# Cross attention scores: 32-row products per head, or 128-row products with zero-padded queries

## The reference

```python
Q = (x_text @ Wq).reshape(Bb, Tt, H, DH)      # H, DH = 4, 32
K = (x_vision @ Wk).reshape(Bb, Gg, H, DH)
scores = jnp.einsum('bthd,bghd->bhtg', Q, K) / np.sqrt(DH).astype(np.float32)
scores = jnp.where(vision_mask[:, None, None, :], scores, -jnp.inf)
topv, topi = jax.lax.top_k(scores, K_TOP)     # K_TOP = 32
probs = jax.nn.softmax(topv, axis=-1)
```

## Time and profile before

| | us |
|---|---|
| median of 3 runs | 5040.57 (5039.6 to 5043.89) |
| profiled execution | 5041.77, of it the span of instructions 5039.7 |
| TensorE busy | 4324.6 (86%), weight loads 3107.2 (62%) |
| VectorE busy | 4096.0 (81%) |
| ScalarE busy | 2074.3 (41%) |
| GpSimd busy | 2188.5 (43%) |
| mean granted TensorE clock | 0.873 |

### The profile page before, as it was taken

The page is one execution under the profiler, slowest core; times in us unless marked ns, Lnnn a source line. Parts: engine busy times, 40 slices in busy tenths (PEclk is TensorE's granted clock), DMA queues, the critical chain, the costliest instruction groups (busy, mean ns, idle before and its releaser), DMA issues. The chain is left out here.

```text
span 5039.7 us, 70649 instructions
## 1 busy us (share of the span) xinstructions
PE 4324.6 (86%) x28037; PEld 3107.2 (62%) x28066; DVE 4096.0 (81%) x4353; ACT 2074.3 (41%) x3688; POOL 2188.5 (43%) x2260
## 2 busy tenths in 40 slices
PE   8999976578889899899899899887578989898984
PEld 6777753256566566566666666667456666666661
DVE  5666659699999999999999999986256767777767
ACT  3433322144444444444444444431234545444453
POOL 1111116434444376677677677660233333333321
PEclk9999988678888788888888888888789999999996
DMA  2111115300001101021101111013531111111101
GB/s 84 51 45 51 49 49 184 120 17 26 31 28 44 45 28 34 30 65 34 32 30 43 57 34 30 28 53 92 194 103 43 61 44 58 47 58 54 51 26 36
DMA packets 214587, 275.98 MB, mean 55 GB/s; under 512 B 96659, under 2 KB 144403, under 8 KB 210224
## 3 DMA queue, kind: packets, MB, share of 16 engines
q1 hardware_dynamic: 196850, 216.91, 14.2%
q0 software_dynamic: 17408, 54.56, 2.9%
HBM read 186.44 MB, written 84.98 MB: 54 GB/s over the span
## 5 line engine op out<-in xcount | busy, mean ns | idle before, releaser
L1548 POOL TENSOR_TENSOR c_s<-c_s,c_z 128x2048 f32<-128x2048 f32 x128 | 581.6, 4544 | 755.6 <-ACT c_z L1333 755.6
L1488 DVE MAX8 c_top<-c_z 128x8 f32<-128x2048 f32 x384 | 878.8, 2288 | 8.8
L1489 DVE MATCH_REPLACE8 c_z<-c_top,c_z 128x2048 f32<-128x2048 f32 x384 | 873.9, 2276 | 0.0
L1174 PEld LDWEIGHTS c_p_a<-c_diag,c_s 128*128 128x128 f32 x4096 | 593.5, 234 | 238.4 <-ACT c_diag L1345 160.6
L1174 PE MATMUL c_p_a<-c_diag,c_s 128*128 128x128 f32 x4096 | 615.8, 321 | 131.3 <-ACT c_diag L1345 95.0
L1164 PE MATMUL c_p_s<-c_kt,c_qT 32*128 32x512 f32 x1024 | 542.4, 920 | 105.1 <-ACT c_s L1327 103.5
L1868 PE MATMUL f_p_g<-f_hT,f_w 128*128 128x128 f32 x4096 | 538.4, 295 | 70.2 <-ACT f_gT L1968 55.7
L1868 PEld LDWEIGHTS f_p_g<-f_hT,f_w 128*128 128x128 f32 x4096 | 526.9, 211 | 90.7 <-ACT f_gT L1968 58.6
L1876 PE MATMUL f_p_o<-f_w,f_gT 128*128 128x512 f32 x1024 | 481.8, 592 | 0.0
L1327 ACT ACTIVATE c_s<-c_p_s 128x512 f32<-128x512 f32 x512 | 286.9, 595 | 362.3 <-PE c_p_s L1165 360.5
L1164 PEld LDWEIGHTS c_p_s<-c_kt,c_qT 32*128 32x128 f32 x1024 | 185.2, 247 | 345.1 <-ACT c_s L1327 321.2
(11 more groups left out here) (360 smaller groups left out, 7561.4 us busy)
## 6 DMA issues: line engine op xcount, KB each, us to landing
mod_out<-c_fo POOLq DMA_DIRECT2D x32, 512.0 KB, 2.9
f_mr<-mod_out SPq DMA_DIRECT2D x32, 512.0 KB, 4.8
p_ct<-in_ctxT SPq DMA_DIRECT2D x16, 768.0 KB, 4.9
c_vals<-in_ctx SPq DMA_DIRECT2D x4, 3072.0 KB, 12.1
c_kb<-kspec SPq DMA_DIRECT2D x22, 512.0 KB, 4.3
a_xt<-in_xT SPq DMA_DIRECT2D x32, 256.0 KB, 3.1
a_xr<-in_x SPq DMA_DIRECT2D x32, 256.0 KB, 2.6
x<-a_out POOLq DMA_DIRECT2D x32, 256.0 KB, 2.5
```

The lines of the kernel that those rows point to most:

```text
L1174: last = mm(p_a[:, n, :], s[:, h, n * P:(n + 1) * P], diag[:, j % 2, :], start=(h == 0 and n % 4 == 0), stop=(h == NH2 - 1 and n % 4 == 3) ...
L1488: st.link(v.max(best[n], z[:, par, :]))
L1489: last = v.match_replace(z[:, par, :], best[n], z[:, par, :], NEG)
L1548: pool.tensor_tensor(s[:, h, :], s[:, h, :], z[:, j % 2, :], ALU.subtract).then_inc(w_ready, 1)
```

## The change

`qT` gets a dimension for the head: `[P, 2, NH2, P]` in place of `[P, 2, P]`. GpSimd clears all of it at the start of the stage, and ScalarE waits for that once. `copy_q` writes each head's 32 rows into that head's own block, with four copies in place of one, so in a block all rows of the other heads stay zero. The scores of a head are then a product over all 128 rows of its block and of `kt`. The mask's product stays as it is.

```diff
-        qT = m.sb("qT", [P, 2, P])
+        qT = m.sb("qT", [P, 2, NH2, P])
...
-                        mm(p_s[:, i, :], qT[r:r + HS, t % 2, :], kt[r:r + HS, cols], start=True, stop=False)
+                        mm(p_s[:, i, :], qT[:, t % 2, 2 * p + i, :], kt[:, cols], start=True, stop=False)
                         mm(p_s[:, i, :], oneb[r:r + 1, :], mrow[r:r + 1, cols], start=False, stop=True).then_inc(s_done, 1)
...
                 act.wait_ge(q_done, t + 1)
-                a(qT[:, t % 2, :], p_m[:, 1, 0:P], ACT.Copy).then_inc(q_copied, 1)
+                for h in range(NH2):
+                    part = slice(HS * h, HS * h + HS)
+                    last = a(qT[part, t % 2, h, :], p_m[part, 1, 0:P], ACT.Copy)
+                last.then_inc(q_copied, 1)
...
+            act.wait_ge(zeroed, 1)
             copy_q(0)
             copy_s(0, 0)
...
         def _(pool):
+            pool.memset(qT[:], 0.0).then_inc(zeroed, 1)
             pool.wait_ge(core_in, 16 * 3)
```

More of the change, by code:

```diff
@@ L964, in cross @@
          prod_ready, v_ready, fb_ready, g_in, ig_in, rf_done, rf_copied, r_step, rk_read, rv_ready, ri_done,
-         ri_copied) = [
+         ri_copied, zeroed) = [
             m.sem(n) for n in (
@@ L971, in cross @@
                 "prod_ready v_ready fb_ready g_in ig_in rf_done rf_copied r_step rk_read rv_ready ri_done "
-                "ri_copied").split()]
+                "ri_copied zeroed").split()]
         cx_in = [m.sem(f"cx_in{u}") for u in range(2)]
```

## The result

The changed kernel takes 5114.86 us (median of 4 runs, 5112.21 to 5118.91) against 5042.23 us before: a ratio of 1.0145, 95% interval 1.0127 to 1.0162. It is slower by 73 us. The forecast was 5041.1 us with a range of 5036 to 5060 us.

A forecast was written before the change was run, and what follows sets the result against it. VectorE's own passes, 18.80 us a head, were taken to bound the stage. The profiled 5041.77 us plus 0.6 for the lead-in gave 5042.4; the runs' median lies 1.2 lower, so 5041.1 us, range 5036 to 5060.

The forecast's parts named there:

- the serial pair: Score products: two heads one after the other take 2.16 us at full clock, 4.3 us at half, before switches.
- Rows of zeros: Score products, rival A: zero rows don't count and the clock still falls; +425 us, 5465 us, chance 0.08.
- The lead-in: Before the stage's first head: first score group ends at 979.1 us, 0.6 us later; bounds 0 to +8.3 us.
- The end: Last attention products after the last score group: 0, up to -4 us if the clock is up.
- The memset: GpSimd's clearing at the stage's start: 0.6 to 4.9 us long, costing 0 in idleness, at dearest under 1.2 us.
- copy_q: ScalarE's query eviction: four copies for one delay the spectra and group 1 by +0.52 us, bounds 0.51 to 0.83.
- The clock afterwards: Score groups: full clock taken from the 128-row streams, so a group lasts 10.93 us, bounds 9.5 to 12.05.
- the cover named for ScalarE: ScalarE behind copy_q: only copy_a and two heads' exponentials, whose buffers VectorE wants most of 18.80 us later.
- starts at 2243.4 us and ends at 2254.4 us: Group 2 of the score products in one tile: ends 2.7 us ahead of VectorE, so VectorE loses nothing.
- The switches: TensorE between 128 rows and one: four a pair at 0.09 us each, bounds 0 to 0.16; pair 2.52 us.
- late from g = 12.3 us on: Score groups: VectorE is late for group 2 once a group's time g reaches 12.3 us.
- Rival B: TensorE's row switches: at 0.25 us each a group takes 13.5 us; +74 us, 5115 us, chance 0.08.

The follow-up runs named there:

- e2: Changed kernel, four copies kept, with the mask's product widened from one row to 128 rows; 5042.0 us, ratio 0.9998.
- e3: Changed kernel with the edits of e1 and e2 together: one copy of the queries and a 128-row mask product; 5042.2 us, ratio 0.9998.
- e1: Changed kernel with one ScalarE copy of the queries again, GpSimd writing the padded blocks from it; 5084.3 us, ratio 1.0075.
- f1: Changed kernel with one copy of the queries releasing TensorE and the four copies into the blocks following on ScalarE; 5070.0 us, ratio 1.0052.
- f3: e1 with the spectra waiting for GpSimd's padding instead of the copy; 5136.0 us, ratio 1.0183.
- e4: Kernel before with only the four copies and zeroed blocks added, products still of 32 rows; 5146.5 us, ratio 1.0202.
- e5: e4 with one copy of the queries releasing TensorE and the four copies following from SBUF, 32-row products; 5074.8 us, ratio 1.0075.
- e8: e1 with ScalarE evicting group 2 before the exponentials of the next head; 5050.2 us, ratio 1.0017.
- e7: e1 with score products of 64 rows, half of them zero, instead of 128; 5412.5 us, ratio 1.0736.
- e6: Kernel before with its copy of the queries cut into two of 64 partitions each; 5056.5 us, ratio 1.0028.

## Why the prediction was wrong

**What held.** VectorE bounds the stage, and nothing counts until a score group is late: wherever no group is late the heads are 18.80 us apart, and e2 and e3, whose groups take very different times on TensorE, end where the kernel before ends. The overlap of the two heads is lost and the serial pair is 2.16 us with wide products alone (e2). Rows of zeros count as rows. The lead-in grew by 0.4 us (from the first product to the first head 13.81 us instead of 13.40), forecast 0.6. The end changed by -2.5 us, within -4 to 0. The memset took 0.95 us and cost nothing visible. (VectorE's digits are 9 from the 9th to the 26th slice, not from the 8th; nothing hangs on it.)

**What failed first: "copy_q", +0.52 us.** Two things. The size was 1.10 - 0.28 = 0.82 us, my upper bound: the copies of a quarter of the partitions are as long as the whole one (268 against 278 ns). And the step counted these copies only as a later start of group 1. They are also idleness of TensorE ahead of the spectra, just behind two other gaps (1.40 and 0.69 us in this tile, as long as before), and it is there that the clock now falls. The runs show it by itself: 0.46 us, no fall in 29 tiles (e1, f1); 1.29 and 1.58 us, 25 to 28 of 29 (changed, e2, f3), and 22 with 32 rows (e4). Where VectorE waited for it, group 1 took up to 17.25 us instead of 10.93. This term carries the 54.4 us ahead of group 1, and all but 1.5 of the 18.6 us ahead of group 2, where TensorE was late already. The part of the prediction that it overturns is "The clock afterwards", where I took full clock from the 128-row streams and never asked what happens at the spectra ahead of them.

**What was wrong second, but cost nothing here: the cover named for ScalarE.** I wrote that only copy_a and exponentials stand behind copy_q. copy_f and group 1's evictions stand there too, with 0.30 us to spare. In the changed kernel TensorE was later still: ScalarE mostly waited 1.39 us for group 1's first product. With 32 rows and no longer gap the same oversight is worth 34 us (e5).

**What was wrong third: group 2 "starts at 2243.4 us and ends at 2254.4 us".** An early start doesn't bring an early end. ScalarE takes up the evictions 11.2 us ahead of VectorE's need at the earliest, and TensorE's waiting for it costs clock as well. The trace of the kernel before shows this already: where its group 2 starts 16 us ahead, at 1188 us for one, it takes 15.5 us and ends 0.60 us ahead of need. In the changed kernel this was hidden, since TensorE mostly came later than ScalarE. e1 shows the price once the gap is gone, 35.7 us, and e8 takes most of it away.

**The switches.** The cost per head was 0.29 us, not 0.18. The way back does cost about what the way there does (0.09 us each), and the second weight load behind a switch is late by another 0.1 us. The group at full clock, 11.58 us, lay inside my bounds (9.5 to 12.05), and by the rule "late from g = 12.3 us on" it would have done no harm. It did harm because the clock took the rest of the room; without the switches a fall at the same place is absorbed (e2).

**Rival B named 5115 us, the time that was measured, but this doesn't make it right.** It put 2.4 us a tile ahead of group 2, at full clock, from 0.25 us a switch. That the sums meet is luck: a switch costs 0.1 us, and three quarters of the waiting is ahead of group 1, at half clock. What it had right is that the one-row products are needed for the loss. No rival was the clock falling somewhere new, and the range, which ended where a group at full clock begins to be late, left it out.

## What to carry to other kernels

The room that an engine off the bound has is shared by all that runs on it. List everything that draws on it (start, length, clock, the evictor's place in its order), and work it out with the worst clock that the neighbouring stretches show, not the best. Compare the sum for a whole tile with what the bound engine takes for one, as lateness is carried into the next tile. A small copy that releases TensorE is priced by the idleness it makes there and by what the clock does after it, not by its own length. If products are padded to all rows, try making the small ones in the same stream as wide as the others; here that alone brought the time back (e2).

## What the runs showed of the hardware

- The rows of a product bear on the granted clock, not only busy time: at the same order of products, 64 rows get 0.59 to 0.67 within groups at 96% busy (e7), 128 rows 1.00 at 94% (group 1 of e1). The Trainium skill, "TensorE: Matmul & The Clock Gate", section "Why this matters for your kernels", names idle gaps alone as what brings the clock down; here the measurement decides.
- Ahead of the spectra (products of 64 columns), behind two other gaps that are 1.40 and 0.69 us in nearly every tile of these runs, 0.46 us of idleness brought a fall in none of the 28 tiles that have this gap (e1), 0.73 us in 5 (e6), 1.29 us in 25 (changed) and 1.58 us in all 28 (f3).
- A one-row product between 128-row products costs 0.29 us each time at full clock. The Trainium skill, "TensorEngine Tiling (Array Packing)", section "Key Properties", says that a change of the tiling mode drains the engine; the traces agree that it costs, with about 0.1 us a switch and 0.1 us for the load behind it.
- After a fall at the spectra, group 1's stream of 128-row f32 products mixed with one-row ones stayed at half clock for up to 12.1 us (2479 to 2491 us in the tile shown); with no one-row products among them, in e2, group 1 stayed there for 5.2 us at most.
